# One VectorE sum for the maximum's rows, the residual sum on GpSimd, and GpSimd's weight split moved to the front of its stage 1

## The reference

```python
x = x + L0_attn(layernorm(x))            # stage 1: linear attention and a GELU MLP
x = x + L0_ffn(layernorm(x))             # stage 2: w1, w2, h1, h2, w3 products
x = x + L3_xattn(layernorm(x), ctx_1024, mask)   # stage 9
# L3_xattn: 16 heads of 16 columns over 4096 keys per batch
scores = einsum('bhqd,bhkd->bhqk', q, k) / sqrt(16)
scores = where(mask, -inf, scores)
ctx = einsum('bhqk,bhkd->bhqd', softmax(scores), v)
```

## Time and profile before

| | |
|---|---|
| median of three runs | 1465.5 us (1463.61 to 1466.17) |
| the profiled execution | 1463.04 us |
| its span, first to last instruction | 1460.9 us |
| PE busy | 1386.2 us (95%) |
| DVE busy | 981.6 us (67%) |
| ACT busy | 797.0 us (55%) |
| POOL busy | 362.6 us (25%) |
| mean granted TensorE clock | 0.987 of full speed |

### The profile page before, as it was taken

The page is one execution under the profiler, slowest core; times in us unless marked ns, Lnnn a source line. Parts: engine busy times, 40 slices in busy tenths (PEclk is TensorE's granted clock), DMA queues, the critical chain, the costliest instruction groups (busy, mean ns, idle before and its releaser), DMA issues.

```text
span 1460.9 us, 24247 instructions
## 1 busy us (share of the span) xinstructions
PE 1386.2 (95%) x9599; PEld 986.7 (68%) x9609; DVE 981.6 (67%) x1627; ACT 797.0 (55%) x1453; POOL 362.6 (25%) x461
## 2 busy tenths in 40 slices
PE   7799989999999999999999989999999998999997
PEld 5788657887898676898566654555555554645797
DVE  5776655334787576787367567989999983566433
ACT  5575335343665364664455426878888885315232
POOL 3685263001633113542101222222121100100000
PEclk9999999999999999999999999999999999999999
DMA  9313215334222433211317174444545304210140
GB/s 373 142 58 130 106 42 179 105 110 176 80 73 109 169 119 123 96 59 57 145 71 263 61 239 165 141 160 131 182 138 174 111 2 187 86 59 1 59 173 15
DMA packets 49071, 177.76 MB, mean 122 GB/s; under 512 B 4864, under 2 KB 6144, under 8 KB 43008
## 3 DMA queue, kind: packets, MB, share of 16 engines
q1 hardware_dynamic: 48960, 176.23, 33.7%
HBM read 132.66 MB, written 44.60 MB: 121 GB/s over the span
## 4 chain that ended last, share of the span: by engine, by line
PE 72%; DVE 15%; ACT 4%; POOL 3%; DMA 3%; issue 2%; SPq 0%; ACTq 0%; POOLq 0%; DVEq 0%
PE PS L160 50%; DVE SM L2397 8%; PE PS L2382 5%; PE PS L2286 4%; PE PS L630 2%; PE PS L2300 2%; DMA CT<-k_tiles 2%; PE PS L1874 1%; PE PS L1895 1%; POOL CNr L1342 1%; PE PS L2961 1%; PE PS L1902 1%; PE PS L2866 1%; DMA k_tiles<-CN 1%; DVE ARr L2414 1%
## 5 line engine op out<-in xcount | busy, mean ns | idle before, releaser
L2397 DVE TENSOR_REDUCE SM<-PS 128x1 f32<-128x1024 f32 x256 | 306.8, 1222 | 31.9 <-PE PS L2286 29.5
L160 PE MATMUL PS<-ARr 128*128 128x256 f32 (+1 forms) x1024 | 271.2, 336 | 0.6 <-POOL CNr L928 0.5
L160 PE MATMUL PS<-CNr,ARr 128*128 128x256 f32 (+1 forms) x952 | 202.1, 320 | 11.7 <-DVE ARr L797 11.4
L160 PEld LDWEIGHTS PS<-ARr 128*128 128x128 f32 x1024 | 181.1, 190 | 18.9 <-issue 0.7
L160 PEld LDWEIGHTS PS<-CNr,ARr 128*128 128x128 f32 x952 | 154.1, 194 | 26.6 <-DVE ARr L797 13.1
L160 PE MATMUL PS<-ARr,HTr 128*128 128x512 f32 x384 | 121.7, 398 | 0.5 <-ACT CN L459 0.5
L2286 PE MATMUL PS<-ARr 64*128 64x512 f32 x320 | 117.1, 448 | 5.1 <-ACT AR L2469 2.8
L858 ACT CAST ARr<-PS 128x512 fp32r<-128x512 f32 x96 | 56.3, 586 | 113.4 <-PE PS L630 113.4
L2300 PE MATMUL PS<-ARr 64*128 64x256 f32 x640 | 116.5, 304 | 1.3 <-DVE ARr L2414 1.0
L2469 ACT ACTIVATE AR<-PS 128x512 f32<-128x512 f32 x172 | 93.5, 605 | 23.4 <-PE PS L2300 14.0
L2469 ACT ACTIVATE CT<-PS 128x512 f32<-128x512 f32 x168 | 91.2, 602 | 18.6 <-PE PS L2300 15.3
(11 more groups left out here) (412 smaller groups left out, 2799.0 us busy)
## 6 DMA issues: line engine op xcount, KB each, us to landing
CT<-k_tiles SPq DMA_DIRECT2D x64, 512.0 KB, 5.0
CN<-ctx_n SPq DMA_DIRECT2D x24, 1024.0 KB, 5.7
k_tiles<-CNr SPq DMA_DIRECT2D x32, 768.0 KB, 3.5
CT<-pack SPq DMA_DIRECT2D x6, 2048.0 KB, 7.6
CT<-ctx_t SPq DMA_DIRECT2D x8, 1024.0 KB, 19.5
k_tiles<-CN SPq DMA_DIRECT2D x32, 256.0 KB, 4.1
AR<-pack SPq DMA_DIRECT2D x16, 512.0 KB, 3.5
v_ones<-CN SPq DMA_DIRECT2D x28, 288.0 KB, 3.2
```

The source lines that it names most:

```text
L160: last = te.matmul(o, l, r, start=first and k == 0, stop=final and k == n - 1, skip_group_check=True)
L2397: ve.tensor_reduce(MX9[:, p % 2, e, g % 2, g % 8 // 2:g % 8 // 2 + 1], PS[:, b:b + 2, :].rearrange("p a b -> p (a b)"), AX, ALU.max).then_inc(
```

## The change

Three edits. In stage 1, GpSimd's program makes the split of stage 2's weights first, not after its sums. In stage 9, the two copies of one row each become one sum over all 128 partitions, bank plus query tile, in place. In stage 9 too, the addition to the residual goes from VectorE to GpSimd, and t9 has two buffers, so VectorE's product waits for the addition of two pairs earlier.

```diff
         def pool_1(pl):
             ge = pl.e
+            weights_pool_1(pl)
             pl.wait_ge(*w1)
...
-            weights_pool_1(pl)
             jobs_pool(pl, "t1b")
...
-        t9 = sm(2, 2, 16)
+        t9 = [sm(2, 2, 16) for _ in range(2)]
...
-                for e in range(2):
-                    r = slice(64 * e + 32, 64 * e + 33)
-                    ve.tensor_copy(QQ9[r, pr, cols], bank("rows", p)[r, 0:256]).then_inc(*dv.inc("turn", "mrow", 9, p))
+                rows = QQ9[:, pr, cols]
+                ve.tensor_tensor(rows, bank("rows", p)[:, 0:256], rows.bitcast(F32), ALU.add).then_inc(
+                    *dv.inc("turn", "mrow", 9, p))
...
-                    dv.wait_ge(("ri", 9, n), ("fin", 9, n - 1) if n else ("row", 9, 3))
+                    dv.wait_ge(("ri", 9, n), ("fin", 9, n - 2) if n > 1 else None)
...
-                    dv.wait_ge(("fin_out", 9, n))
-                    ve.tensor_tensor(x, x, t9.rearrange("p i e r -> p i (e r)"), ALU.add).then_inc(
-                        *dv.inc("mixed", "fin", 9, n))
...
+                if what == "finish":
+                    b2, pr, _ = of_pair(n)
+                    x = X[:, 2 * b2:2 * b2 + 2, 32 * pr:32 * pr + 32]
+                    pl.wait_ge(("fin_out", 9, n), ("fin", 9, n - 1) if n else ("row", 9, 3))
+                    pl.e.tensor_tensor(x, x, t9[n % 2].rearrange("p i e r -> p i (e r)"), ALU.add).then_inc(
+                        *pl.inc("mixed", "fin", 9, n))
```

More of the change, by code:

```diff
@@ L2438, in dve_9 @@
                     ps = bank("fin", n)[:, 0:68].rearrange("p (i e r) -> p i e r", i=2, e=2)
-                    x = X[:, 2 * b2:2 * b2 + 2, 32 * pr:32 * pr + 32]
                     dv.wait_ge(("fin_ps", 9, n), ("fin_out", 9, n - 1) if n else None)
                     ve.reciprocal(ri9[:, n % 2], ps[:, :, :, 16]).then_inc(*dv.inc("mixed", "ri", 9, n))
-                    dv.wait_ge(("ri", 9, n), ("fin", 9, n - 1) if n else ("row", 9, 3))
-                    ve.tensor_tensor(t9, ps[:, :, :, 0:16], ri9[:, n % 2].unsqueeze(3).to_broadcast([128, 2, 2, 16]),
+                    dv.wait_ge(("ri", 9, n), ("fin", 9, n - 2) if n > 1 else None)
+                    ve.tensor_tensor(t9[n % 2], ps[:, :, :, 0:16], ri9[:, n % 2].unsqueeze(3).to_broadcast([128, 2, 2, 16]),
                                      ALU.mult).then_inc(*dv.inc("mixed", "fin_out", 9, n))
-                    dv.wait_ge(("fin_out", 9, n))
-                    ve.tensor_tensor(x, x, t9.rearrange("p i e r -> p i (e r)"), ALU.add).then_inc(
-                        *dv.inc("mixed", "fin", 9, n))
                     if n == 15:
```

## The result

The changed kernel takes 1456.32 us in the median of four runs (1454.65 to 1458.65), the kernel before 1465.15 (1463.61 to 1466.17, four runs). The ratio is 0.9942 with a 95% interval of 0.9924 to 0.9959: 8.8 us faster by the medians, 6.0 to 11.1 by the interval, with 7.9 forecast; the predicted 1457.6 is 1.3 us too high.

The account below looks back on a forecast made before the run. TensorE was taken to set stage 9's pace, and GpSimd's late weight split to hold up stage 2. Terms of -5.2, +0.4, -3.4 and +0.3 made -7.9 us, from 1465.5 to 1457.6 us; range 1454.5 to 1460.

Parts of the forecast that it names:

- The tail of stage 1 to stage 2: From stage 1's end to stage 2's first product, moving GpSimd's weight split forward saves 5.2 us (2.7 to 6).
- Rival A: TensorE's clock falls anyway in stage 2's new gap, so the early split saves only 2.7 to 3.2 us; chance 0.14.
- The head of stage 1: At stage 1's start, the moved split may hold VectorE's norm instructions L299; costs 0.4 us, bounds 0 and 1.7.
- Rival C: GpSimd's split at stage 1's front holds VectorE on the path, PSUM-fed instructions too: slower, 1467 us; chance 0.06.
- Stage 9: One sum for two copies frees the score bank sooner, so TensorE waits less: 3.4 us saved.
- the last pair: At stage 9's end TensorE waits 0.97 us after the transposes; the one sum takes away 0.46 of it.
- The 13 places: Stage 9's steps after the transposes lose their whole bank wait, 0.19 us each, 2.5 us together.
- The statistics pair: In stage 9's pair with batch 0's statistics the bank comes 0.46 us earlier; the rest of TensorE's wait stays.
- Rival B: Stage 9's longer step is TensorE's own refilling after the transposes, so only 0.46 us is gained there; 1460.5 us; chance 0.06.
- The residual sum: Moved to GpSimd in stage 9, it saves nothing in the loop and costs 0.3 us at the end, up to 1.3.
- Rival D: In stage 9, GpSimd's addition for finish 7 is caught behind a late key DMA; 1458.8 us if 3 us late; chance 0.06.

Follow-up runs that it names:

- the run with three: The changed kernel with two copies of the bank into unread tiles ahead of each new sum; 1460.83 us, ratio 0.9984.
- the run with the signal moved: The kernel before, split still late, with the signal that GpSimd's stage 1 has ended given ahead of the split; 1465.28 us, ratio 1.0007.

## Why the prediction was right

- *The tail of stage 1 to stage 2.* Forecast -5.2, measured -5.40 (-5.42 with the front move alone). Each link came as worked out, shifted by the 2.08 us of the late start: L294 4.94 us earlier (4.87 forecast), the transposes 4.59 (4.4), the first product 4.79 (4.73). To this last number I had added 0.45 for that product's half-clock duration. It took 1.07 and now takes 0.47, so the term is 0.60, and 4.79 + 0.60 = 5.39 is the whole distance.
- *Rival A, the clock.* It did not fall in the new gap, and stood at 1.00 through 1.22 us of idling. All six profiled kernels with the split in front keep the upper level from stage 1 into stage 3, and in all four with the split late it falls, at 216.4 to 218.9. So the outcome is no accident of one execution. But the row that I had put against it, 0.97 us at the last pair, was a weaker argument than I took it for, since in this same trace the clock is at half from 138.3 on, right behind two shorter gaps:

```profile
135.94 0.66 PE L630 MATMUL PS<-CST,AR 128*128 128x128 f32 x4 [0.91 <-ACT AR L867]
...
137.49 2.30 PE L160 MATMUL PS<-CNr,ARr 128*128 128x256 f32 x12 [0.90 <-DVE ARr L797]
```

The length of one gap alone didn't decide what the clock did; my argument from it came out in part by luck.

- *The head of stage 1.* Forecast +0.4, measured 0. The four L299 took 3.97 us where I had bounds of 3.5 and 5.2, and TensorE's jobs hid all of it. *Rival C* fell by the same rows: L366 with one input in PSUM was not held.
- *Stage 9.* Forecast -3.4 (of it 0.46 in the last pair), measured -3.24 in the loop and -0.45 in the last pair, -3.69 together. The 13 places gave 0.20 to 0.22 each, 2.7 together, where I had 0.19 and 2.5. The statistics pair was the term too small: 2.17 to 1.59 is 0.58, not 0.46. Its two copies, in the kernel before:

```profile
1074.45 0.88 DVE L2414 CAST ARr<-PS 1x256 fp32r<-1x256 f32 x2
```

They began 0.03 us after the maximum ahead of them had ended (1074.42) and 1.14 after TensorE's step; the sum began 0.08 before its maximum's end (1072.36) and 1.03 after the step. So it saves 0.11 at its start as well. In the middle pair the same 0.11 is there (0.41 and 0.30 after the step), but TensorE's own 1.24 hides it. In the last pair VectorE stands idle before either, and the gain is 0.45. *Rival B* fell with the one sum alone: the steps went to 1.24.
- *The residual sum.* Forecast +0.3, measured +0.13: GpSimd took 0.32 (0.3 taken), and product to statistics is 0.66 us where it was 0.52. I had charged two handings over at 0.13; the rows show 0.09 and 0.03. *Rival D* had 1.43 us of room left and didn't come.

Together -5.4 + 0 - 3.7 + 0.13 = -9.0, against -7.9 forecast: the signs of all terms but the head's are as forecast, and the miss of 1.1 lies in the head (0.4), the tail (0.2), the statistics pair and the loop (0.3), and the handing over (0.2). All four err to the same side, so the total is 1.1 short. The run times, with an interval of 5 us, could not have told 7.9 from 9.0; the distances do. The 1455.1 that I gave for the profiled execution was missed, at 1458.65: I had carried over a difference of 2.5 us between the median and the profiled execution, and that difference is a matter of where the clock falls in one execution.

## What to carry to other kernels

When an engine's wait names another engine, ask also what that engine's work does to instructions beside it: here, in the traces, signalling earlier gave 2.2 us and moving the work gave 5.4, and in the run times the first gave nothing that can be told. Compare two executions by distances between the same instructions, stage by stage; the spans differed by 4.0 us where the change was worth 9.0. And to show that a buffer's release sets a pace, hold it beyond the pace by a measured margin, since a dose that stays under it looks like a refutation.

## What the runs showed of the hardware that I had not expected

- Two instructions of VectorE on all 128 partitions overlap: the second started 0.08 us before the first's end (1006.92 against 1006.59 + 0.41), and so in the run with three. A chain of n of this size costs about 0.33 n + 0.08 us, not 0.41 n; the four L1215 at 219.35, of 0.42 each, took 1.42.
- Copies of one partition are dearer than they look. The pair took 0.88, without overlap, and began 0.03 us after the end of the instruction before; one instruction on all 128 partitions took 0.41 and began 0.08 before that end. The copies start at partitions 32 and 96 and also have another form, and no run tells which of these it is.
- Beside a train of GpSimd's instructions on SBUF, a VectorE TENSOR_SCALAR on SBUF can wait for one of them to end, however small it is: 128 x 4 went from 0.17 to 1.12, 128 x 256 from 0.41 to between 0.70 and 1.43. Not every VectorE instruction on SBUF is held. In the run with the signal moved, the statistics L304 at 214.83 took 0.43 beside the same train, what they take elsewhere.
- One half-clock stretch costs about 1.5 us here: from stage 3's norm to stage 4's it is 132.84 with one and 131.3 without. Such stretches go with most of the 10 us by which the runs of one kernel differ. The kernel before took 1458.02 us at a mean granted clock of 0.986 and 1468.75 at 0.979 on one chip, 1459.27 at 0.986 and 1469.90 at 0.979 on the other; 0.007 of 1461 us is 10.2 us.
